# Zeros of unowned rows sent by the sync engine in six parts, and unread bf16 products at TensorE's waits in the second cross attention

## The reference, cut to what matters

```python
# layer 1, cross attention: 16 heads of 16, 77 keys
attn = jnp.einsum('bhqd,bhkd->bhqk', q, k) * scale
attn = jnp.clip(attn, -CLAMP, CLAMP)          # CLAMP = 10000.0
attn = jax.nn.softmax(attn, axis=-1)
x = jnp.einsum('bhqk,bhkd->bqhd', attn, v).reshape(B, Nq, Cq)
return x @ Wo + bo
...
# layer 1, experts: a row that no token owns counts as nothing
buf = jnp.zeros((E, cap + 1, H), dtype=x.dtype).at[a_e, p].set(x_a)
contrib = y[a_e, p] * (a_w * valid.astype(x.dtype))[:, None]
```

## Time and profile before

| what | value |
|---|---|
| runs | 1277.59 us median of 3 (1275.09 to 1281.85) |
| the profiled execution's own time | 1270.34 us |
| its span, first to last instruction | 1268.3 us |
| PE busy | 1009.9 us (80%) |
| DVE busy | 578.7 us (46%) |
| ACT busy | 356.5 us (28%) |
| POOL busy | 228.8 us (18%) |
| mean granted clock of PE | 0.892 |

### The profile page before, as it was taken

How to read it: one execution, slowest core, us unless ns; L and a number is a source line. 1 busy time by engine, 2 the same in 40 slices (tenths; PEclk the granted TensorE clock), 3 DMA queues, 4 the chain that set the end, 5 groups by cost and what they waited for, 6 DMA issues and landing times.

```text
span 1268.3 us, 19930 instructions
## 1 busy us (share of the span) xinstructions
PE 1009.9 (80%) x8500; PEld 761.2 (60%) x8500; DVE 578.7 (46%) x1328; ACT 356.5 (28%) x491; POOL 228.8 (18%) x234
## 2 busy tenths in 40 slices
PE   6889689889888888887875797988879797974860
PEld 3656566656657777776874564756556474643540
DVE  3544343545683411111113825565473649445227
ACT  2344324433442121111110153242315322430112
POOL 0310210210302222323221010101010110102642
PEclk9899789988988999999997897999699789966995
DMA  5012912012005778767662000200020010004426
GB/s 168 2 38 97 347 42 67 1 38 67 1 1 215 282 282 303 269 249 258 253 254 83 1 6 2 67 2 5 1 67 2 5 34 1 2 1 128 148 90 198
DMA packets 68216, 129.22 MB, mean 102 GB/s; under 512 B 12752, under 2 KB 57696, under 8 KB 63136
## 3 DMA queue, kind: packets, MB, share of 16 engines
q1 hardware_dynamic: 45984, 97.85, 22.5%
q10 hardware_dynamic: 16480, 14.62, 3.6%
q0 software_dynamic: 5664, 15.47, 3.4%
HBM read 94.50 MB, written 33.42 MB: 101 GB/s over the span
## 4 chain that ended last, share of the span: by engine, by line
PE 52%; DVE 22%; DMA 13%; ACT 6%; POOL 2%; issue 2%; SPq 1%; ACTq 1%; DVEq 0%; POOLq 0%
DMA sb_arena<-in_m_w 11%; PE ps L1627 7%; PE ps L1324 6%; PE ps L1443 6%; DVE sb_arena L793 6%; PE ps L1509 4%; PE ps L1419 4%; ACT sb_arena L587 4%; DVE sb_arena L797 3%; PE ps L1637 3%; DVE ps L816 3%; PE ps L1562 3%; PE ps L1465 2%; PE ps L1701 2%; PE ps L1451 2%
## 5 line engine op out<-in xcount | busy, mean ns | idle before, releaser
L1627 PE MATMUL ps<-sb_arena 128*128 128x128 f32 x1248 | 161.1, 284 | 44.0 <-DMA sb_arena<-in_m_w 43.3
L1627 PEld LDWEIGHTS ps<-sb_arena 128*128 128x128 f32 x1248 | 151.4, 198 | 56.9 <-DMA sb_arena<-in_m_w 55.6
L1214 POOL TENSOR_TENSOR sb_arena<-sb_arena,sb_neghalf 128x2 f32<-128x2 f32 x40 | 30.5, 762 | 602.4 <-DVE sb_arena L759 602.4
L587 ACT ACTIVATE sb_arena<-ps 77x2048 f32<-77x2048 f32 (+1 forms) x64 | 118.4, 1875 | 54.6 <-PE ps L1401 42.0
L1324 PE MATMUL ps<-sb_arena,sb_wreg 128*128 128x256 f32 (+1 forms) x512 | 107.9, 363 | 4.6 <-issue 3.8
L1324 PEld LDWEIGHTS ps<-sb_arena,sb_wreg 128*128 128x128 f32 (+1 forms) x512 | 89.2, 195 | 19.7 <-issue 8.3
L1419 PE MATMUL ps<-sb_arena 32*77 32x256 f32 (+1 forms) x1024 | 92.5, 491 | 7.7 <-ACT sb_arena L587 4.9
L1112 DVE COPY sb_arena<-ps 128x256 f32<-128x256 f32 x39 | 16.6, 424 | 161.2 <-PE ps L1621 161.2
L822 DVE RECIPROCAL sb_arena<-ps 128x32 f32<-128x32 f32 x24 | 8.6, 357 | 147.0 <-PE ps L1451 146.0
L1637 PE MATMUL ps<-sb_arena 128*128 128x256 f32 x312 | 73.9, 380 | 0.6 <-ACT sb_arena L688 0.6
L1273 POOL DMA_INDIRECT outs<-sb_arena,sb_idx x39 | 38.3, 983 | 196.4 <-ACT sb_arena L688 196.4
(11 more groups left out here) (228 smaller groups left out, 1710.1 us busy)
## 6 DMA issues: line engine op xcount, KB each, us to landing
sb_arena<-in_m_w SPq DMA_DIRECT2D x39, 1536.0 KB, 7.1
sent<-sb_xres SPq DMA_DIRECT2D x32, 256.0 KB, 2.9
sb_arena<-outs SPq DMA_DIRECT2D x16, 512.0 KB, 5.8
outs<-sb_zeros ACTq DMA_DIRECT2D x1, 6656.0 KB, 32.7
sent<-sb_zeros ACTq DMA_DIRECT2D x2, 2560.0 KB, 12.7
sb_arena<-in_m_w SPq DMA_DIRECT2D x16, 256.0 KB, 3.7
early<-sb_xres SPq DMA_DIRECT2D x12, 256.0 KB, 2.9
sb_arena<-in_xT SPq DMA_DIRECT2D x8, 256.0 KB, 3.3
```

The lines of the kernel that those rows point to most:

```text
L587: nc.scalar.activation(dst, src, ACT.Exp).then_inc(S(f"h_PT{p}"), 1)
L1627: ins = mm(to[:, m * P:(m + 1) * P], w[:, k, m * P:(m + 1) * P], slots0[j % 2].xT[:, k, :], start=(k == 0), stop=(k == KC - 1))
```

## The change

Two edits that have nothing to do with each other:

- The stage `clear` and its three transfers leave ACT's list. SP starts six transfers instead, two behind the sends of each of the first three pairs: `sent0` and `sent1` (2560 rows each), then `outs1` in four parts of 1664 rows. POOL waits for six instead of three.
- A function `idle` issues products of 128 x 32 weights (columns 96 to 127 of the bf16 identity) with 512 columns of a constant bf16 tile. They write partitions 96 to 127 of `bank(p, 0)`. The transposed scores of `X1` use partitions 0 to 76 alone, so nobody reads them. Four stand ahead of p = 0's wait for the split maxima. At every clip wait (two k, two p) there are four for p = 0 and six for p = 1. That makes 24 products a pair, 96 in all.

```diff
+IDLE, IDLE_SPLIT, IDLE_CLIP = 96, 4, (4, 6)
+FILL = (PICKS + E * CAP) // 4
...
-                          {"g_dec": [("clear",)]} if n == 1 else {})
+                          {})
...
+            fills = [sent0[PICKS:, :], sent1[PICKS:, :]] + [outs1[FILL * k:FILL * (k + 1), :] for k in range(4)]
+
+            def fill(rows):
+                sp.dma_start(rows.rearrange("(t p) d -> p t d", p=P), zeros[:, :].unsqueeze(1).broadcast_to([P, rows.shape[0] // P, D])
+                             ).then_inc(S("cleared"), 16)
...
                 for p in range(2):
                     send(p, n - 1, 0)
+                for rows in fills[2 * n - 2:2 * n]:
+                    fill(rows)
...
-            def clear(p, n):
-                for rows in (sent0[PICKS:, :], sent1[PICKS:, :], outs1):
-                    act.dma_start(rows.rearrange("(t p) d -> p t d", p=P), zeros[:, :].unsqueeze(1).broadcast_to([P, rows.shape[0] // P, D])
-                                  ).then_inc(S("cleared"), 16)
...
-            play(order0, stages | {"clear": clear, "raw": lambda p, n: picks(1, 1)})
+            play(order0, stages | {"raw": lambda p, n: picks(1, 1)})
...
-                    pool.wait_ge(S("cleared"), 16 * 3)
+                    pool.wait_ge(S("cleared"), 16 * 6)
...
+            def idle(p, count):
+
+                for _ in range(count):
+                    mm(bank(p, 0)[IDLE:P, :], identb[:, IDLE:P], headrow[:, :, :].rearrange("p g k -> p (g k)"), start=True, stop=True)
+
             def shift_rows(p, n, c):
+                if c is X1 and p == 0:
+                    pe.wait_ge(S(f"h_max{p}"), c.scores_at(n) + c.score_units)
+                    idle(p, IDLE_SPLIT)
...
             def shift(p, n, c, k):
+                idle(p, IDLE_CLIP[p])
                 pe.wait_ge(S(f"h_clip{p}"), KC * n + k + 1)
```

## The result

The changed kernel takes 1238.03 us, median of 4 runs (1232.22 to 1240.83). The kernel before took 1279.72 beside it (4 runs, 1275.09 to 1284.14). The ratio is 0.966, with 95% between 0.9633 and 0.9688: faster by 3.4%. Set against the 1277.59 of the prediction this is 1234 us. The forecast was 1246, and the range ended at 1238. The direction and both mechanisms were right; the gain was larger than the range allowed.

The account below looks back on a forecast made before the run. No engine was taken as the bound as a whole; each edit was priced at its own place, by the delay the next engine sees. 10.7 + 21 = 31.7 us off 1277.59 gave 1245.9, forecast 1246, range 1238 to 1260.

Parts of the forecast that it names:

- the comparison with pair 2: First layer, decay's first instruction to gated output: pair 1 takes 26.32 us, pair 2 without zeros 15.58, difference 10.7.
- the zeros' term: Pair 1 of the first layer: moving the zeros from ACT to SP saves 10.7 us, bounds 7.5 and 10.7.
- The products' term: X1 in four pairs: unread products hold PE's clock and save 20.8 us, rounded to 21; bounds 0 and 23.
- Values to output product: X1: these stages at full instead of half clock save 3.95 us a pair, 15.8 over four pairs.
- 0.35 is given back: X1: second p's exponential comes 2.20 us behind the first, half the values needs 1.85, so 0.35 is lost per pair.
- the late shifts: X1, clips of k = 1: the products for p = 0 exceed its wait; 0.3 us lost a pair, 1.2 in all.
- Transposed scores to values: X1: scores ahead of each clip save 7.2 us, less 1.2 for late shifts and 1 for clock falls in the scores.
- The check on PE's share: X1, one k of 5.9 us or so: PE busy 0.73 of the time with the products, beside 0.79 in S1.
- Products that queue without holding the clock: Rival at X1's clip waits: products late by 4.5 us a pair, 18 over four; 1284.9 us, chance 0.10.
- The clock holding in some pairs only: Rival in X1: the clock may fall in the scores, leaving half of 21 us; 1256.4 us, chance 0.14.
- The zeros' gain given back: Rival: transfers delay something behind SP, or the next wait replaces the stall; 1256.6 us, chance 0.05.
- Neither hold nor cost: Rival at X1: the products neither hold the clock nor cost anything; 1266.9 us, chance 0.03.

Follow-up runs that it names:

- The kernel with fewer products at k = 1: Changed kernel with the four split products also in X0 and S1, and two products fewer at each clip of k = 1: 1232.32 us, 0.9679 of before.
- the doubled kernel: Changed kernel with twice the unread products, eight at the split, eight and twelve at the clips: 1248.14 us, ratio 0.9837 to the kernel before.
- short products: Changed kernel with unread products of 128 columns instead of 512, same number and places: 1254.42 us, 0.985 of the kernel before by the medians.

## Why the prediction was right in kind and too small

**The zeros' local gain: right.** The place gave 10.75 us for the 10.7 of the comparison with pair 2. The lower bound of 7.5, and the 8.7 of the issue alone, are out. The Trainium skill's rule (page "DMA: Bandwidth & Descriptors", section "Issuing engines are not separate DMA queues") that another issuer saves the issuing time alone describes the transfers rightly, since they moved as many bytes and showed no cost on SP; the 2 us beyond it came from PE, which no longer sits through the stall: its clock is 1.00 behind the decay, where it was 0.50.

**The step that failed: the zeros' term, "The bounds are 7.5 us, the one long issue alone, and 10.7. I take 10.7".** As an upper bound 10.7 was wrong, and with it the lower end of the range. Alone, the move measured 16.3 us, with 95% from 11.1 to 21.3. Eight profiled kernels have the zeros on SP and no products in the first layer, and their pairs 1 to 3 take from 264.4 to 274.9 us, with a mean of 270.9 (266.3, 266.3, 274.9, 274.3, 274.9, 274.8, 264.4, 271.4). The three with the zeros on ACT take 283.2 in the mean (282.8, 282.8, 284.1). The difference is 12.3, and single profiles lie between 8 and 19 from that mean. By pairs the 12.3 are 10.6 in pair 1, 0.3 in pair 2 and 1.4 in pair 3. So 10.7 was right as the mean of what pair 1 gives, and what the term left out is 1.7 us in the pairs behind it and, above all, the spread: with the zeros on SP pair 2 takes 88.7 or 88.8 us in three of the eight profiles and 92.2 in five, at the same work and two shares of half clock. The term should have been some 12, from 8 to 19. Whether the stall on ACT makes the longer kind likelier behind it stays open: with the zeros on ACT pair 2 took 90.5 twice and 92.65 once.

**The products' term: right, with two small errors against each other.** Forecast 20.8, measured 22.7 alone (18.6 to 26.8). By the rows of the four pairs in the two first profiles:

- Values to output product: forecast 15.8. Before, 48.4 in all: 12.11, 12.37, 12.33, 11.54. After, 30.4: 7.61, 7.60, 7.61, 7.61. Saved 17.9. The "0.35 is given back" did not occur. ACT's timeline shows the last two exponentials back to back, x2 in 3.64 us from 979.61, since the first of them is late: its clip, the first half of the 4.49 us from 976.12, is done at about 978.4, and its shift starts at 979.14, behind the four products. The give-back and the late shifts were one effect, and the sum counted it twice. The kernel with fewer products at k = 1 bears this out: without the late shift, 0.19 us is given back.
- Transposed scores to values: forecast 7.2 less 1.2 and less 1. Before 14.25 in pair 2; after 12.51 in the pairs that start at full clock and 13.41 in those that start at half. Over four pairs (13.83, 14.25, 14.25, 14.25 to 13.41, 12.51, 13.41, 12.51) 4.7 saved, for 5.0 forecast.
- The check on PE's share had its own slips: its four terms give 4.23 of 5.9 us, 0.72 and not 0.73, and the scores and shifts of both p were put at 1.7 and 0.4 us, where the rows show 1.97 and 0.84. PE is busier than forecast, 5.03 of the 6.00 us from 860 to 866 in pair 1. This changes no term of the sum.

ACT's timeline in `X1` of pair 2 after the change, the exponentials of k = 1:

```profile
979.61 3.64 ACT L597 ACTIVATE sb_arena<-ps 77x2048 f32<-77x2048 f32 x2 [2.52 <-PE ps L1414]
```

**The rivals.** Products that queue without holding the clock: not here, at 24 a pair; the doubled kernel shows the queue, 14.4 us dear, with the clock held. The clock holding in some pairs only: the fall in the scores did come, in two pairs of the changed kernel's first profile and in all four of its second, where the prediction looked for one or two. But some microseconds into the stage the clock was back, and with 512 columns it then stayed in all eight; with 128 it stayed in some only. The zeros' gain given back: no, and no loss is shown with twice the zeros either. Neither hold nor cost: no.

**The range.** Its lower end came from "10.7 + 23" and "a few microseconds of luck with the clock". The changed kernel's runs spread over 8.6 us in one set and 13.2 in the other, and the two profiles of the changed kernel differ by 8.4 us of span with no change in code. Of these 8.6 lie in the first layer's pairs and 4.6 between the values, and -4.7 in the rest. There the first profile has one late expert in the last layer, PE's timeline:

```profile
1161.25 4.67 PE L1715 MATMUL ps<-sb_arena 128*64 128x256 f32 x12 [3.94 <-issue]
```

Five of the thirteen profiles have such a wait, of 3.9 to 5.4 us, with and without the products. The two measurements put the kernel at 0.970 x 1277.59 = 1239 and at 0.966 x 1277.59 = 1234, one just inside the range and one outside, so the miss itself is within the spread between measurements; with the zeros' term bounded at 19 and the rest as it was, the range would have reached 1230.

**What stays open.** The rows explain 12.3 + 22.6 = 34.9 us, the single edits timed give 39.0, the whole change timed gives 38 and 42. The intervals touch, so a further gain of 3 to 7 us outside the two places is neither shown nor excluded.

## What to carry to other kernels

Look for chains of short waits in which PE is at half clock although it is mostly busy, and price them by the same stages at full clock elsewhere in the trace; unread products that just fit into such a wait can keep the clock once it is back, and those beyond the wait make the next product late (here 0.15 us for each of 96 more). A DMA issue that holds its queue for microseconds belongs on an engine whose queue nobody waits for. And the same loop can take more or less of its time at half clock from one execution to the next, so the range has to hold that spread beside the bounds of the terms.

## What was unexpected of the hardware

- The clock fell without a long wait. Before the change the longest wait of PE around its fall in `X1` was 2.10 us, and 22.28 of 27.30 us of work at half clock did not lift it. In three pairs it came back and fell again at the end of a wait of 1.78 us. With the split's four products alone it fell at the end of the second of two waits, 1.55 and 1.78 us. The Trainium skill, page "TensorE: Matmul & The Clock Gate", section "A second HAM failure mode: psum-queue depth-cycling", tells of another kernel in which short idle times between groups of matmuls make the clock go up and down; this trace agrees.
- Products that nobody reads count. Four of 512 columns take 1.04 us at full clock, and with ten of them in each clip round the clock, once back, stayed in every pair. With ten of 128 columns the values ran at full clock in two pairs of four.
- The same loop body takes 88.8 or 92.2 us from one execution of the same program to the next. It often keeps to its kind, as in the changed kernel's second profile, where pairs 1 and 2 took 92.25 and 92.21, but not always: with short products pair 2 took 92.18 and pair 3 87.01, which is the length of the shorter kind there.
- PE's writes to partitions 96 to 127 of a bank whose partitions 0 to 76 belong to the running clip on DVE cost DVE nothing: the two clips take 4.49 us after the change, as before. The clip covers four banks, and no row tells in which of them DVE is at a given moment, so it is not shown that both were in one bank at once.

```profile
970.20 4.49 DVE L821 TENSOR_SCALAR ps<-ps 77x2048 f32<-77x2048 f32 x2 [2.46 <-PE ps L1432]
```
